# Cross-attention and routed feed-forward on one core: the block diagonals copied for two batches at a time, the row maxima carried as two rows of them

## The reference

```python
x = x + xattn(layernorm(x), ctx, ctx, mask, Wq, Wk, Wv, Wo)
x = x + ffn(layernorm(x), wg, w1, w3, w2)

# xattn
scores = einsum('bhqd,bhkd->bhqk', Q, K) / sqrt(8); scores = where(mask == 0, -1e9, scores)
out = einsum('bhqk,bhkd->bhqd', softmax(scores), V);  out @ Wo.T
# ffn
probs = softmax(x @ wg.T); topk_w, topk_idx = top_k(probs, 2); topk_w /= sum(topk_w)
y = einsum('tei,ehi->teh', silu(x @ w1[e].T) * (x @ w3[e].T), w2);  out = sum of expert_w * y
```

## Time and profile before

| what | value |
|---|---|
| three runs | 285.69, 286.79, 287.94 us (median 286.79) |
| span of the profiled execution | 289.2 us |
| PE matmul / weight load | 220.1 us (76%) / 161.4 us (56%) |
| DVE | 214.5 us (74%) |
| ACT | 131.9 us (46%) |
| POOL | 109.8 us (38%) |

### The profile page before, as it was taken

One profiled execution on the slowest core, in us unless ns is written; L12 is line 12 of the kernel. 1 busy time (PEld: TensorE's weight loads), 2 busy tenths in 40 slices (PEclk: granted clock), 3 DMA queues, 4 the chain that ended last, 5 costly groups with the idle time before them and its releaser, 6 DMA issues.

```text
span 289.2 us, 5289 instructions
## 1 busy us (share of the span) xinstructions
PE 220.1 (76%) x1445; PEld 161.4 (56%) x1445; DVE 214.5 (74%) x619; ACT 131.9 (46%) x291; POOL 109.8 (38%) x120
## 2 busy tenths in 40 slices
PE   0787779998989988887667674688787789997620
PEld 0663456666757665665336542477566668886410
DVE  4779966688759867895977786568895568775596
ACT  5777127554665448342145546243334435453300
POOL 4310350121403070105486556104556565555530
PEclk9996579999999999979756799589899999999855
DMA  6954411353033302331602110421342232211807
GB/s 216 318 233 118 131 35 28 92 125 86 9 98 96 94 0 67 87 100 47 207 9 67 46 39 29 99 47 30 77 79 76 82 84 73 80 52 26 236 5 217
DMA packets 38108, 26.33 MB, mean 91 GB/s; under 512 B 4748, under 2 KB 35726, under 8 KB 37696
## 3 DMA queue, kind: packets, MB, share of 16 engines
q1 hardware_dynamic: 34848, 19.76, 25.5%
q0 software_dynamic: 2656, 5.40, 6.1%
q10 hardware_dynamic: 576, 0.83, 0.9%
HBM read 12.32 MB, written 6.31 MB: 64 GB/s over the span
## 4 chain that ended last, share of the span: by engine, by line
PE 42%; DVE 30%; issue 10%; SPq 8%; DMA 4%; ACT 2%; POOL 1%; another core or an unknown queue 1%; DVEq 0%; ACTq 0%; POOLq 0%
SPq L427 8%; PE bank L528 8%; DVE m_neg L1411 6%; PE bank L759 4%; PE bank L760 3%; PE bank L733 3%; PE bank L652 3%; DMA bd<-st 3%; PE bank L746 3%; PE bank L736 3%; PE bank L693 2%; PE bank L676 2%; PE bank L734 2%; PE bank L679 2%; PE bank L534 2%
## 5 line engine op out<-in xcount | busy, mean ns | idle before, releaser
L1411 DVE TENSOR_REDUCE m_neg<-bank 128x4 f32<-128x512 f32 x64 | 43.5, 684 | 15.4 <-PE bank L693 15.0
L1048 POOL DMA_INDIRECT ys<-big x39 | 38.1, 976 | 40.0 <-DVE big L1447 19.2
L923 ACT ACTIVATE big<-bank 128x512 f32<-128x512 f32 x64 | 37.4, 597 | 20.9 <-PE bank L679 20.0
L797 ACT ACTIVATE st<-bank 128x128 fp32r<-128x128 f32 (+1 forms) x78 | 22.6, 330 | 31.6 <-PE bank L746 16.1
L1004 POOL DMA_INDIRECT xg<-rows,rows_i x24 | 24.6, 1027 | 31.8 <-DVE rows_i L1218 11.6
L693 PE MATMUL bank<-bd,st 128*128 128x512 f32 x64 | 31.1, 509 | 4.7 <-DMA bd<-st 3.8
L676 PE MATMUL bank<-m_bd,ones_b 128*128 128x512 f32 x64 | 31.3, 489 | 2.1 <-ACT big L923 1.9
L759 PE MATMUL bank<-bd,st 128*128 x78 | 24.3, 332 | 9.8 <-DVE big L1447 6.2
L1355 DVE SCALAR_TENSOR_TENSOR st<-st_hi,cst,bank 128x512 fp32r<-128x512 f32 x32 | 23.3, 747 | 11.3 <-ACT st_hi L797 9.0
L1026 POOL TENSOR_TENSOR m_bd<-mT,cst 128x512 fp32r<-128x512 f32 x16 | 17.3, 1110 | 30.1 <-DVE mT L1334 30.0
L679 PE MATMUL bank<-bd,st 128*128 128x512 f32 x64 | 27.1, 423 | 0.0
(11 more groups left out here) (174 smaller groups left out, 514.0 us busy)
## 6 DMA issues: line engine op xcount, KB each, us to landing
bd<-st SPq DMA_DIRECT2D x126, 64.0 KB, 2.0
big<-xg SPq DMA_DIRECT2D x39, 64.5 KB
raw<-in_L_ffn_w SPq DMA_DIRECT2D x2, 1024.0 KB, 9.3
raw<-ys SPq DMA_DIRECT2D x6, 256.0 KB
x_all<-in_x SPq DMA_DIRECT2D x4, 256.0 KB, 4.5
rows<-in_mask_BxS_if POOLq DMA_DIRECT2D x4, 256.0 KB, 5.2
ctx_all<-in_L_ffn_w SPq DMA_DIRECT2D x1, 1024.0 KB
ctx_all<-in_ctx SPq DMA_DIRECT2D x3, 256.0 KB, 5.2
```

What stands on the lines that cost most here:

```text
L923: nc.scalar.activation(prob[n % 2][:, NJ * g:NJ * (g + 1), :].rearrange("p h q -> p (h q)"), s2[k % 2][:, :], ACT.Exp, scale=SCALE).then_i ...
L1048: pool.indirect_dma_start(ys, bass.IndirectOffsetOnAxis(xt[n % XR][:, D:RW].bitcast(I32), 0), y_sb[n % YR], None, bounds_check=PAIRS - 1, ...
L1411: nc.vector.tensor_reduce(m_neg[:, H * (b - 1) + NJ * g:H * (b - 1) + NJ * (g + 1)], s1[k % s1_ring(u)][:, :].rearrange("p (j q) -> p j q" ...
```

## The change

Each side gets four buffers of block diagonals (eight in all, laid out with j outside the groups), and the stacks are laid out by batch. One transfer now copies rows 0 to 25 of one head range for two batches; four transfers make the diagonals of two batches (diagonals). Key stacks carry a 1 at partitions 26 and 27, which the query diagonals meet with two whole rows of maxima, high and low parts; SP copies these from mT, two transfers for two batches (maxima_rows). The product L676, ones_b, m_bd and GpSimd's masks are removed. SP's order in a stage becomes: the maxima rows of the stage before, two pairs of key diagonals, two pairs of query diagonals. raw13 holds one weight: w1 is loaded early, w2 and then w3 in stage 4 behind the maxima rows, w3 when w1 has been split; the pieces are taken in the order w1, w2, w3.

```diff
+USED = 26
+MROWS = 2
+MAX = USED
...
+    c[:, C_ONE_K] = (p == MAX) | (p == MAX + 1)
+    c[:, C_CK] = np.where((r >= 8) & (r < 16), -1.0, 0.0) + c[:, C_ONE_K]
...
-        st = sb("st", [P, 2, 2, NG, T], F32R)
-        bd = sb("bd", [P, 6, NG * NJ * P], F32R)
+        st = sb("st", [P, 2, 2, QB, NG, P], F32R)
+        bd = sb("bd", [P, 2 * QB, NG * NJ * P], F32R)
...
-        m_hl = sb("m_hl", [P, 2, QB * H])
-        mT = sb("mT", [P, P])
-        m_bd = sb("m_bd", [P, H, P], F32R)
+        m_hl = sb("m_hl", [P, 2, 2, 2 * H])
+        mT = sb("mT", [P, P], F32R)
...
-        raw = [raw13[:, 0, :], raw13[:, 1, :], ctx_all[:, :, :].rearrange("p b d -> p (b d)")]
+        raw = [raw13[:, :], ctx_all[:, :, :].rearrange("p b d -> p (b d)"), raw13[:, :]]
...
+        def diagonal_blocks(k, m, j):
+
+            u, h = divmod(m, 2)
+            rows = slice(R * j, R * j + USED)
+            slot0 = QB * (1 - k) + 2 * h
+            return (bd[rows, slot0:slot0 + 2, NG * P * j:NG * P * (j + 1)].bitcast(F32),
+                    st[rows, u % 2, k, 2 * h:2 * h + 2, :, :].rearrange("p b g c -> p b (g c)").bitcast(F32))
...
-            def block_diagonal(k, n):
-
-                u, b = divmod(n, QB)
-                stacks_in(sp, u, k)
-                if n >= 3:
-
-                    sp.wait_ge(s1_full if k else s2_full, NG * (n - 2))
...
+            def diagonals(k, m):
+
+                stacks_in(sp, m // 2, k)
+                if m >= 2:
+
+                    sp.wait_ge(s1_full if k else s2_full, NG * 2 * (m - 1))
                 else:
-                    sp.wait_ge(bd_cleared, 3 if k else 6)
-                for j in range(2 if k and n == 0 else NJ):
-                    rows = slice(R * j, R * (j + 1))
-                    sp.dma_start(bd_slot(k, n)[rows, :, j, :].bitcast(F32), st[rows, u % 2, k, :, b * S:(b + 1) * S].bitcast(F32)
-                                 ).then_inc((kbd_ready if k else qbd_ready)[n % 3], 16)
+                    sp.wait_ge(bd_cleared, (0 if k else QB) + 2 * (m + 1))
+                for j in range(2 if k and m == 0 else NJ):
+                    sp.dma_start(*diagonal_blocks(k, m, j)).then_inc((kbd_ready if k else qbd_ready)[m % 2], 16)
+
+            def maxima_rows(m):
+
+                u, h = divmod(m, 2)
+                taken(sp, ("MT", u))
+                if m >= 2:
+                    sp.wait_ge(s2_full, NG * 2 * (m - 1))
+                else:
+                    sp.wait_ge(bd_cleared, QB + 2 * (m + 1))
+                for a in range(2):
+                    sp.dma_start(bd[MAX + a:MAX + a + 1, QB + 2 * h:QB + 2 * h + 2, :].rearrange("p s (m q) -> p (s m) q", q=P).bitcast(F32),
+                                 mT[4 * H * h + 2 * H * a:4 * H * h + 2 * H * (a + 1), :].bitcast(F32)).then_inc(mrow_ready[h], 16)
 
             for u in range(NQ + 1):
+                if u:
+                    maxima_rows(2 * (u - 1))
+                    maxima_rows(2 * (u - 1) + 1)
                 if u == NQ:
                     sp.wait_ge(work_full, slot["V", NQ - 1] + 1)
                     sp.wait_ge(ck_ready, NQ)
-                    sp.dma_start(raw[2], w2).then_inc(in_w2, 16)
-
-                for k, b in ((1, 0), (1, 1), (1, 2), (0, 3), (1, 3)):
...
+                    sp.dma_start(raw[1], w2).then_inc(in_w2, 16)
+                    sp.wait_ge(wlo_ready, NB // 4)
+                    sp.dma_start(raw[2], w3).then_inc(in_w3, 16)
                 if u < NQ:
-                    block_diagonal(0, QB * u)
-                    block_diagonal(0, QB * u + 1)
-                    block_diagonal(0, QB * u + 2)
+                    for k in (1, 0):
+                        diagonals(k, 2 * u)
+                        diagonals(k, 2 * u + 1)
...
-                            if g == 0:
-                                diagonal_in(pe, 0, n)
+                            if g == 0 and b % 2 == 0:
+                                diagonal_in(pe, 0, n // 2)
+                                maxima_in(pe, n // 2)
                             if k >= 2:
                                 pe.wait_ge(prob_ready, k - 1)
...
-                            if b == 0:
-                                pe.wait_ge(mbd_ready, NG * (u - 1) + g + 1)
-                            nc.tensor.matmul(s2[k % 2][:, :], ones_b[:, b, :],
-                                             m_bd[:, NJ * g:NJ * (g + 1), :].rearrange("p h q -> p (h q)"),
-                                             start=True, stop=False)
...
+                            nc.tensor.matmul(s2[k % 2][:, :].rearrange("p (j q) -> p j q", j=NJ), st[:, (u - 1) % 2, 1, b, g, :],
+                                             bd_slot(0, n)[:, g, :, :], start=True, stop=True).then_inc(s2_full, 1)
...
-                                diagonal_in(pe, 1, n)
+                                if b % 2:
+                                    diagonal_in(pe, 1, n // 2)
...
-                    act.wait_ge(in_w13, 32)
+                    act.wait_ge(in_w1, 16)
                     act.wait_ge(s1_full, NG * B)
+                if k == NB // 4:
+                    act.wait_ge(in_w2, 16)
                 if k == NB // 2:
-                    act.wait_ge(in_w2, 16)
+                    act.wait_ge(in_w3, 16)
                     act.wait_ge(s2_full, NG * (B - 2))
...
-                        if is_k:
-                            i = copy(st_hi[:, n % SH, :], src)
-                        else:
-                            i = nc.scalar.activation(st_hi[:, n % SH, :], src, ACT.Identity, bias=cst[:, C_ONE:C_ONE + 1])
-                        i.then_inc(sthi_ready, 1)
+                        one = C_ONE_K if is_k else C_ONE
+                        nc.scalar.activation(st_hi[:, n % SH, :], src, ACT.Identity, bias=cst[:, one:one + 1]).then_inc(sthi_ready, 1)
...
-                    for k in (3, 4, 5):
+                    for k in range(3, 2 * QB):
                         clear_diagonal(k)
...
-                    for g in range(NG):
-                        nc.gpsimd.tensor_tensor(m_bd[:, NJ * g:NJ * (g + 1), :], mT[:, :].unsqueeze(1).to_broadcast([P, NJ, P]),
...
-            def ones_b_columns():
-                nc.vector.tensor_copy(ones_b[:, :, :], cst[:, C_BATCH:C_BATCH + QB].unsqueeze(2).to_broadcast([P, QB, P])
...
-                            nc.vector.tensor_reduce(m_neg[:, H * (b - 1) + NJ * g:H * (b - 1) + NJ * (g + 1)],
+                            nc.vector.tensor_reduce(m_neg[:, H * (b - 1) + g:H * b:NG],
```

More of the change, by code:

```diff
@@ L293, in program @@
         y_sb = [space[:, 2048 + k * D:2048 + (k + 1) * D] for k in range(YR)]
+        got = [r.rearrange("p (b d) -> p b d", b=B) for r in (raw13[:, :], space[:, 6144:8192])]
         acc = [space[:, 4 * I + k * D:4 * I + (k + 1) * D] for k in range(2)]
@@ L345, in program @@
         bd_cleared = sem("bd_cleared")
-        kbd_ready = [sem(f"kbd_ready{k}") for k in range(3)]
-        qbd_ready = [sem(f"qbd_ready{k}") for k in range(3)]
+        kbd_ready = [sem(f"kbd_ready{k}") for k in range(2)]
+        qbd_ready = [sem(f"qbd_ready{k}") for k in range(2)]
+        mrow_ready = [sem(f"mrow_ready{k}") for k in range(2)]
         s1_full, max_done = sem("s1_full"), sem("max_done")
@@ L377, in stacks_in, with diagonal_in, maxima_in @@
                     taken(engine, ("st", u, k))
-        def diagonal_in(engine, k, n):
-            engine.wait_ge((kbd_ready if k else qbd_ready)[n % 3], 16 * NJ * (n // 3 + 1) - (32 if k and n % 3 == 0 else 0))
-            if k and n == 0:
+        def diagonal_in(engine, k, m):
+            engine.wait_ge((kbd_ready if k else qbd_ready)[m % 2], 16 * NJ * (m // 2 + 1) - (32 if k and m % 2 == 0 else 0))
+            if k and m == 0:
                 engine.wait_ge(first_half, 32)
+        def maxima_in(engine, m):
+            engine.wait_ge(mrow_ready[m % 2], 16 * MROWS * (m // 2 + 1))
+        def diagonal_blocks(k, m, j):
[4 more added lines that the diff above has]
+                    st[rows, u % 2, k, 2 * h:2 * h + 2, :, :].rearrange("p b g c -> p b (g c)").bitcast(F32))
         x_d = x.rearrange("(u b) s d -> u s b d", b=QB)
@@ L720, in turn_tile @@
                 nc.tensor.transpose(tb[n % 2], xt[n % XR][:, 0:D], ident).then_inc(t_full, 1)
-            first_high = bd[:, 0:3:2, :]
-            first_low = [wt_lo[k].rearrange("p k c -> p (k c)") for k in range(2)]
-            second = bd[:, 4:6, :]
+            first_high = bd[:, 0:5:4, :]
+            first_low = [w.rearrange("p k c -> p (k c)") for w in (wt_lo[0], w3_lo)]
+            second = bd[:, 2:4, :]
             def hidden(n):
@@ L1325, in _ @@
             split_tokens(0)
-            ones_b_columns()
             for u in range(NQ + 1):
@@ L1345, in _ @@
                         dve.wait_ge(s2_full, NG * QB * (u - 1))
-                        for n in range(QB * (u - 1) - 3, QB * (u - 1)):
-                            diagonal_in(dve, 1, n)
-                            diagonal_in(dve, 0, n)
```

(3 more changed lines are left out.)

79 lines of the change are left out of this document (26 added, 53 removed).

## The result

The changed kernel is slower: a median of 292.89 us (291.07 to 295.14, four runs) against 287.37 for the kernel before on the same chip; the ratio is 1.0186, 95% interval 1.0107 to 1.0265. On another chip, later, it was 293.07 against 288.56: 1.0126 (1.0067 to 1.0185). The forecast was 285.0, with a range from 281.2 to 288.5.

The account below looks back on a forecast made before the run. PE was taken to bound b = 1 to 3 of stages 1 and 2, the key diagonal's landing b = 0; 2.0 + 2.0 + 1.2 + 0.5 - 0.8 - 0.1 = 4.8, less 3.0 for the clock, gave 285.0 us (281.2 to 288.5).

Parts of the forecast that it names:

- What bounds the kernel: PE sets the pace in b = 1 to 3 of stages 1 and 2, the key diagonal b = 0; stage 4 mostly waits.
- The product: Removing the L676 matmuls from PE gains 2.0 us each in stages 1 and 2, 1.2 in stage 3, 0.5 in stage 4.
- the signs: Signs of being right: b = 1 to 3 of stages 1 and 2 in about 12 us, about 13.5 with a cold start.
- Two batches per transfer: Key diagonals at the head of stages 1 to 3: 106 KB takes 0.46 us, so the last lands 0.18 us later.
- The rival with the 26-row transfers: Transfers occupying engines over 0.65 us delay key diagonals by 12 x (T - 0.65) over three stages: 290.4 us, chance 0.12.
- The clock: With b = 0 losing half its matmuls, b = 1 starts at 1.2 GHz in two of three stages, losing 3.0 us.
- The fall of the earlier trace: Kernel before: PE busy 1.68 of 3.70 us from 121.9 to 125.6, then granted 0.50; taken as agreeing with the skill.
- The maxima rows: Hidden behind stacks in stages 1 to 3; in stage 4 first exponential about 0.7 us later with 0.4 spare: cost nothing.
- The weights: In stage 4, w2 lands at 154.4, before the fifth weight copy at 156.06, hidden by 1.7 us; w3 has slack.
- the key copies: ACT's key copies take 690 instead of 600 ns, 0.09 us before the last key stack.
- the clears: Two more clears of 1.9 us each lie hidden in ACT's wait before 35.21; uncovered they would cost 3.8 us.
- The base: Profiled span 289.2 us against median 286.79; differences taken as equal in both, so 286.79 - 1.8 = 285.0.

Follow-up runs that it names:

- the clock held and 32 rows: Changed kernel with 32 rows per transfer instead of 26 and four extra matmuls at the end of b = 0 of stages 1 to 3: 285.58 us, ratio 0.9869.
- the product back: Kernel with 32 rows, one extra matmul shaped like L676 ahead of each of the 64 second scores: 291.90 us, ratio 1.0082 to the kernel before.
- 32 rows: Changed kernel with every block diagonal transfer copying all 32 rows instead of 26, no extra matmuls: 289.82 us, ratio 1.0029 to the kernel before.
- GpSimd's issues: Changed kernel with 32 rows, GpSimd issuing the third and fourth transfer of the first key pair in stages 1 to 3: 289.96 us, ratio 1.0072.
- the first transfer kept small: Kernel with 32 rows and four extra matmuls, first key pair of stages 1 to 3 sent batch by batch (64 KB): 282.42 us, ratio 0.9778.

## Why the prediction was wrong

**What bounds the kernel: right.** PE's pace in b = 1 to 3 of stages 1 and 2, the landing of the key diagonal in b = 0, and PE waiting in stage 4 (sixteen extra matmuls there made it only 0.5 us longer) all held.

**The product: right in stages 1 and 2, and in part luck in the sum.** The terms were 2.0, 2.0 and 1.2. With the clock held and 32 rows, b = 1 to 3 of stages 1 and 2 took 11.7 us each, where the signs named about 12, and VectorE took over as forecast (7.90 of 8.20 us). Over b = 1 to 4 stages 1 to 3 gained 1.5, 1.5 and 1.9 us, 5.0 instead of 5.2. The third is not shown to be the product's: putting the product back cost 1.5 us in stage 1 and 0.3 in stage 3 (27.59 against 27.32). The prediction did not see the bound of the old transfers: with them the next wait behind PE is for the diagonals, as the run without the product shows. Since the change halves SP's issues, the sum did not suffer.

**Two batches per transfer: the step that failed.** It read "that is under the 0.65 between issues, so issue still sets the pace and the last of the four lands 0.18 later". It took the issue's own duration from transfers of 32 rows and changed only the data. With 26 rows the issue itself went from 0.60 to 0.83 us. Three longer gaps (3 x 0.26 = 0.8) and a tail of 2.52 instead of 2.04 us (0.5) make the 1.2 to 1.3 us of stages 1 and 3; stage 2 has 0.4 more from the gap on SP. 4.3 us in three stages stand where 0.5 stood. The rival with the 26-row transfers had the right place and sign, at a chance of 0.12, but it priced how long a transfer occupies the engines, where the runs show the time that SP takes to issue it. (Nor does a transfer touch half of the partitions: it is 26 of 128.) Its formula, 12 x (0.91 - 0.65), gives 3.1; it left out the tail. Size is the lesser part: with 32 rows, twice the data of before, the landing is 1.7 us later in three stages, of which 0.5 are the gap in stage 2.

The Trainium skill ("DMA: Bandwidth & Descriptors", section on why a DMA increments its semaphore by 16) counts 13 engines for 26 rows. It adds that the issuing engine itself writes the missing part of the count at once. The trace agrees: the semaphore of such a transfer rises in one early step and 13 later ones (stage 1: 47.76, then 48.67 to 49.06), that of a 32-row transfer in 16. That the 0.2 us of longer issue are this write is a guess; no run separates it from the row count.

**The clock: right in kind, wrong in its condition and too small.** "two of the three stages: 2 x 1.5 = 3.0" became three stages and 5.5 us (65.3 against 59.8). The price of one fall was right: in stage 1 it is 1.5 us (17.47 against 15.94). In the changed kernel b = 1 to 3 took 13.2 and 13.8 us, where the signs named about 13.5 for a cold start. But all three stages fell, and stages 2 and 3 for longer (2.1 and 1.9 us). The step argued that b = 0 "keeps its length but loses half its matmuls" and that this is enough. Its length was what changed, and the kernel without the product, with such a b = 0 at its old length, kept 1.00 in the first steps b = 1 of its profile. By one profile each, the falls at the head of stages 1 to 3 are: none at the old landing of 4.2 us, with the product or without; at 4.6 to 5.1 us none or one with the product (before with 26 rows; the product back) and two without it (32 rows; GpSimd's issues); three, and longer, at 5.5 to 5.9; none where four or eight matmuls fill the wait. A late landing was paid again in the clock, and that coupling is what the prediction lacked. The Trainium skill ("TensorE: Matmul & The Clock Gate", section on HAM oscillation) describes bursts that go cold because of the wait for a transfer between them; the trace of the changed kernel agrees, with a wait of 2.23 us that ends at 51.94 and the fall behind it. The fall of the earlier trace rows, which the prediction also took as agreeing, agrees only in that PE waited between bursts: it waited for VectorE (1.73 us before its matmul at 123.58), not for a transfer.

**The maxima rows: wrong by 0.7 to 1.1 us in stage 4.** "Cost nothing" set 0.4 us of spare time on ACT and DVE against a delay of 0.7; the first exponential came 1.0 us later, and leaving the rows out shortened the stage by 0.7 to 1.1. The stage as a whole, from the copy's end to the first product with the experts' weights, took 39.0 us against 39.1 before, where 0.5 was to be gained. In stages 1 and 3 the rows are hidden, as said.

**The weights, the key copies and the clears: right.** w2 had landed at the fifth copy, ACT's copies into st_hi took 690 ns in the mean, as said, and two more clears do not show: the copy of the maxima that ends stage 0 came at 38.7 and 40.3 us in the two profiles of the changed kernel, at 39.4 before. What the end of GpSimd's masks is worth no run shows by itself.

**The base.** "differences are taken as equal in both" failed by 4 us in the other direction for the spans: the profile of before had a slow routed part, so span against span is 1.4 us where the medians are 5.5 apart. The 4.6 us lost ahead of the routed part are most of these; where the rest lies is not settled.

Put together for stages 1 to 3 of the trace: forecast 5.2 gained, 0.5 lost in landing (and 0.3 before it, in the key copies), 3.0 lost in the clock. Measured 5.0 gained (with both defects removed), 4.3 lost in landing, and 6.1 lost in b = 1 to 4 against that kernel (65.3 less 59.2), all but 0.6 of it the clock.

## What to carry to other kernels

When a transfer changes its shape, its issue is a cost of its own: take it from a row with the same count of rows, and treat a count that is not a multiple of 16, where none is in the trace, as unknown on both sides. Where an engine that is kept at its fast clock only by work waits for a transfer, removing work from that stretch and delaying the transfer make each other worse (here no fall or one with either alone, two or three with both); a few matmuls into a bank that is overwritten anyway cost nothing there. A removed bound is worth only what the next one allows: the product alone gave 0.4 us, with the halved issues and the clock held 3 to 4, and with the first transfer kept small 6.

## What the runs showed of the hardware

SP's issue of a transfer with 26 rows took 0.81 to 0.90 us at the head of stages 1 to 3, with pieces of 512 B (52 KB) as with 2 KB (104 KB); with 32 rows it took 0.53 to 0.71, for 64 as for 128 KB. GpSimd's issue of the same 26-row transfer in stage 0 took 0.63 and 0.59 us. Four 128 KB transfers issued by two queues within 1.1 us landed no earlier than from one queue over 2 us (last landing 4.5 and 4.4 us after the first issue). Lifting TensorE's granted clock of stage 4 from 0.59 to 0.67 (before the change it was 0.76) with sixteen extra matmuls did not shorten the stage (39.4 and 39.9 us).
